# Attention in a hybrid block: turned probabilities copied out of PSUM once, low parts on GpSimd, wide score copies, heads in one stream

## The chip, the cores and the metric

The kernel runs on one core of one Trainium2 chip. The metric is the device time of one execution in microseconds. A profiled execution gives a page and a trace of one run; times inside it are counted from the start of its span. Abbreviations: PE is TensorE's matmuls and PEld its weight loads, DVE is VectorE, ACT is ScalarE, POOL is GpSimd, SP is the engine that issues DMAs.

## The reference

The whole program is a grouped convolution with attention, then a state-space block with a dense and a routed feed-forward part. The change touches only attention over the 4096 pixels of an image, in 8 heads (2 images x 4 groups) of 64 channels:

```
# qn (gated, normalized input), key_ and value: (b, g, 64, 4096) each
qf = jnp.transpose(qn.reshape(b, g, cq, h * w), (0, 1, 3, 2))
kf = jnp.transpose(key_.reshape(b, g, cq, h * w), (0, 1, 3, 2))
vf = jnp.transpose(value.reshape(b, g, cq, h * w), (0, 1, 3, 2))
scores = jnp.einsum('bgnc,bgmc->bgnm', qf, kf) * (1.0 / math.sqrt(c))   # c = 256
attn = jax.nn.softmax(scores, axis=-1)
ctx = jnp.einsum('bgnm,bgmc->bgnc', attn, vf)
```

## The kernel before

The convolution phase leaves q, k and v in DRAM, split into bf16 parts that add up to nearly f32. `attention_phase` works through 8 heads, each cut into 32 query tiles of 128 queries (`g` counts tiles over all heads). A tile has 4096 scores per query.

Scores: for each of 8 chunks of 512 keys three bf16 matmuls (L534) add up q times k in a PSUM bank of `ps_s`, which has four. VectorE copies a chunk to `prob[u]` in SBUF (L615), scaled by 1/16, and takes the chunk's maximum; after eight chunks L620 takes the negated row maximum. ScalarE takes the exponentials in place, 1024 columns at a time, with their sums (L586). `prob` has two buffers, for tiles in turn (`u`).

Values: TensorE needs the probabilities turned, keys on the partitions. For each of 8 groups `k` of 512 keys, four f32 transposes go to one of two PSUM banks `ps_t` (L543). ScalarE copies the group as bf16, the high part `hi` (L592); VectorE subtracts the high part from PSUM and writes the rest as bf16, the low part `lo` (L624). Then four pairs of matmuls (L554) take high and low parts as weights: the high part against 128 columns of `vv` (both bf16 parts of v), the low part against 64. At the end of a tile VectorE sums and inverts the row sums (L628, L630), adds the two halves of `ps_o` and scales them (L633, L635) into `oh`, which SP stores for each head.

The order on each engine is written out by hand. In round `k` of a tile, TensorE does the scores of the next tile (chunks 0 and 1 in round 0, then one chunk in rounds 1 to 6: `SCORES_AT`), the values of group `k - 2`, and the transposes of group `k`. VectorE does the score copies, in round 6 the maximum, the low part, and in round 2 the finish of the tile before. ScalarE does the high part and, after rounds 0, 2 and 4, the tile's next exponentials, after round 6 the first of the next tile. The transposes of group `k` wait for exponential `k // 2` and for the low part of group `k - 2`, whose bank they overwrite. Every head begins with its eight score chunks and a maximum, then runs its 32 tiles, and ends with its last values and finish before the next head's scores start.

Of the kernel before, what the change touches and what calls it, by code (L numbers as in the profile page):

```python
# [13 lines left out]
P = 128  # L14
# [429 lines left out]
def attention_phase(nc, ctx, ident, q_split, k_split, v_split, attn_out):  # L444

# [8 lines left out]
    hi, lo = sb("p_hi", [P, 2, CH], BF16), sb("p_lo", [P, 2, CH], BF16)  # L457
    mx, nmx = sb("mx", [P, 2, NCH]), sb("nmx", [P, 2])
# [3 lines left out]
    ps_s = ctx.enter_context(nc.psum_tensor("ps_s", [P, 4, CH], F32))  # L462
# [5 lines left out]
    t_ready, hi_ready, lo_ready, pv_done = sem("t_ready"), sem("hi_ready"), sem("lo_ready"), sem("pv_done")  # L468
    o_ready, o_stored, fin_step = sem("o_ready"), sem("o_stored"), sem("fin_step")

    LOADS = 11
    SC = L // CH
    EC = SC // 2
    TG = L // CH
    scale = 1.0 / 16.0


    SCORES_AT = (0, 0, 1, 2, 3, 4, 5, 6)

# [4 lines left out]
    def tiles(eng, head, step):

        step(head * QT, 0, 0, False, True)
        with eng.Fori(0, QT // 2 - 1) as it:
            for u in (1, 0):
                step(head * QT + it * 2 + 2 - u, it * 2 + 2 - u, u, True, True)
        step(head * QT + QT - 1, QT - 1, 1, True, False)  # L490

    def heads(eng, body):
        with eng.Fori(0, HEADS // 2) as hp:
            for j in range(2):
                body(hp * 2 + j, j, hp)

    start_semaphores()
    with nc.Block() as block:
        @block.sync
        def _(sp):  # L500
# [26 lines left out]
        @block.tensor  # L527
        def _(pe):
            def head(h, j, hp):
                def scores(g, t, u, c):  # L530

                    pe.wait_ge(s_copied, ONE + g * SC + c + 1)
                    for n, (a, b) in enumerate(((qa, ka), (qa, kb), (qb, kc))):
                        last = pe.matmul(ps_s[:, c % 4, :], a[j][:, ds(t * P, P)], b[j][:, c * CH:(c + 1) * CH],  # L534
                                         start=(n == 0), stop=(n == 2))
                    last.then_inc(s_ready, 1)

                def transposes(g, t, u, k):

                    pe.wait_ge(exp_ready, ONE + g * EC + k // 2 + 1)  # L540
                    pe.wait_ge(lo_ready, ONE + g * TG + k + 1)
                    for m in range(4):
                        last = pe.transpose(ps_t[:, k % 2, m * P:(m + 1) * P],  # L543
                                            prob[u][:, (4 * k + m) * P:(4 * k + m + 1) * P], ident[:, :])
                    last.then_inc(t_ready, 1)

                def values(g, t, u, k):

                    pe.wait_ge(lo_ready, ONE + g * TG + k + 3)
                    if k == 0:  # L550
                        pe.wait_ge(o_ready, ONE + g)
                    for m in range(4):
                        for n, (part, cols) in enumerate(((hi, P), (lo, DH))):
                            last = pe.matmul(ps_o[:, u, 0:cols], part[:, k % 2, m * P:(m + 1) * P], vv[j][:, 4 * k + m, 0:cols],  # L554
                                             start=(k == 0 and m == 0 and n == 0), stop=(k == TG - 1 and m == 3 and n == 1))
                    last.then_inc(pv_done, 1)

                def step(g, t, u, before, after):
                    for k in range(TG):
                        if after:  # L560
                            for c in range(SC):
                                if SCORES_AT[c] == k:
                                    scores(g + 1, t + 1, 1 - u, c)
                        if k >= 2:
                            values(g, t, u, k - 2)
                        elif before:
                            values(g - 1, t - 1, 1 - u, TG - 2 + k)
                        transposes(g, t, u, k)
                    if not after:
                        values(g, t, u, TG - 2)  # L570
                        values(g, t, u, TG - 1)

                pe.wait_ge(loaded[j], ONE + (hp + 1) * 16 * LOADS)
                for c in range(SC):
                    scores(h * QT, 0, 0, c)
                tiles(pe, h, step)

            heads(pe, head)

        @block.scalar  # L580
        def _(act):
# [7 lines left out]
            def his(g, k):  # L589
                act.wait_ge(t_ready, ONE + g * TG + k + 1)  # L590
                act.wait_ge(pv_done, ONE + g * TG + k + 1)
                act.activation(hi[:, k % 2, :], ps_t[:, k % 2, :], ACT.Copy).then_inc(hi_ready, 1)  # L592

            def step(g, t, u, before, after):
                if not before:
                    exps(g, u, 0)
                for k in range(TG):
                    his(g, k)
                    if k in EXPS_AT:
                        c = EXPS_AT.index(k) + 1  # L600
                        if c < EC:
                            exps(g, u, c)
                        elif after:
                            exps(g + 1, 1 - u, 0)

            act.preload_act_table(ACT.Exp)
            heads(act, lambda h, j, hp: tiles(act, h, step))

        @block.vector
        def _(dve):  # L610
            def head(h, j, hp):
                def copies(g, u, c):

                    dve.wait_ge(s_ready, ONE + g * SC + c + 1)
                    dve.tensor_scalar(prob[u][:, c * CH:(c + 1) * CH], ps_s[:, c % 4, :], scale, -FLT_MAX,  # L615
                                      ALU.mult, ALU.max, accum_out=mx[:, u, c:c + 1]).then_inc(s_copied, 1)

                def maximum(g, u):
                    dve.wait_ge(s_copied, ONE + g * SC + SC + 4)
                    dve.tensor_reduce(nmx[:, u:u + 1], mx[:, u, :], AX.X, ALU.max, negate=True).then_inc(max_ready, 1)  # L620

                def los(g, u, k):
                    dve.wait_ge(hi_ready, ONE + g * TG + k + 1)
                    dve.tensor_tensor(lo[:, k % 2, :], ps_t[:, k % 2, :], hi[:, k % 2, :], ALU.subtract).then_inc(lo_ready, 1)  # L624

                def finish(g, t, u):

                    dve.tensor_reduce(rsum[:, u:u + 1], rs[:, u, :], AX.X, ALU.add).then_inc(fin_step, 1)  # L628
                    dve.wait_ge(fin_step, ONE + g * 3 + 1)
                    dve.reciprocal(rinv[:, u:u + 1], rsum[:, u:u + 1]).then_inc(fin_step, 1)  # L630
                    dve.wait_ge(fin_step, ONE + g * 3 + 2)
                    dve.wait_ge(pv_done, ONE + (g + 1) * TG + 2)
                    dve.tensor_scalar(otmp[:, :], ps_o[:, u, DH:P], rinv[:, u:u + 1], None, ALU.mult).then_inc(fin_step, 1)  # L633
                    dve.wait_ge(fin_step, ONE + g * 3 + 3)
                    dve.scalar_tensor_tensor(oh[:, j, ds(t, 1), :].rearrange("p a c -> p (a c)"), ps_o[:, u, 0:DH],  # L635
                                             rinv[:, u:u + 1], otmp[:, :], ALU.mult, ALU.add).then_inc(o_ready, 1)

                def step(g, t, u, before, after):
                    for k in range(TG):
                        if after:  # L640
                            for c in range(SC):
                                if SCORES_AT[c] == k:
                                    copies(g + 1, 1 - u, c)
                        if after and k == MAX_AT:
                            maximum(g + 1, 1 - u)
                        los(g, u, k)
                        if before and k == FINISH_AT:
                            finish(g - 1, t - 1, 1 - u)
                    if not after:
                        finish(g, t, u)  # L650

                if j == 0:
                    dve.wait_ge(o_stored, ONE + hp * 32)
                for c in range(SC):
                    copies(h * QT, 0, c)
                maximum(h * QT, 0)
                tiles(dve, h, step)


            dve.sem_inc(s_copied, 4)  # L660
            dve.sem_inc(lo_ready, 2)
            dve.sem_inc(pv_done, 2)
            dve.sem_inc(o_ready, 1)
            heads(dve, head)


# [1580 lines left out]
```

## Time and profile before

| | |
|---|---|
| median of 3 runs | 9130.96 us (9113.76 to 9133.64) |
| the profiled execution | 9120.24 us, span 9118.2 us |
| mean granted TensorE clock | 0.948 |
| busy over the span: TensorE, VectorE, ScalarE, GpSimd | 89%, 76%, 56%, 42% |
| attention, in the profile | from about 658 to 3847 us |

The page shows the busy share of each engine over the whole span and the costliest groups of instructions. "idle before" is the time that an engine stood still ahead of the instructions of a group, and behind the arrow is what ended it. Matmuls are pipelined: one that lasts 0.22 us can start 0.08 us after another, so distances between starts say more about TensorE than durations do.

### The profile page before, as it was taken

To read this page: it belongs to the slowest core of one execution; us is meant where nothing else is said; L and a number is where in the kernel's file an instruction comes from. 1 tells how busy PE (TensorE), PEld (TensorE's weight loads), DVE (VectorE), ACT (ScalarE), POOL (GpSimd) and SP (SyncE) were. 2 spreads that over 40 slices of the span, in tenths; PEclk is the share of its full clock that TensorE was granted. 3 is DMA by queue.
4 is the path that set the end of the run, shared out by engine and by line. 5 is a ranking of instruction groups with operands and counts; after the bars stand their busy time and mean duration, and the time that the engine had idled before them with its cause. 6 is when DMAs were issued, how large, how long until landed. Compare 5 with 4: busy or idle time off the path is not lost. (4 is left out here: it accounts for less than half of the span.)

```text
span 9118.2 us, 145832 instructions
## 1 busy us (share of the span) xinstructions
PE 8092.2 (89%) x44996; PEld 4779.7 (52%) x44996; DVE 6910.1 (76%) x11667; ACT 5070.7 (56%) x8536; POOL 3849.0 (42%) x1769
## 2 busy tenths in 40 slices
PE   8969999999999999858999999999999998684993
PEld 3436666666666666633444444444444443353883
DVE  3428888888888888748998899899999999561116
ACT  2227777777777777635666666666556665221223
POOL 1000000000000000019999999999999999332005
PEclk9989999999999999969999999999999999897996
DMA  1130101011010100041111111111111111233213
GB/s 66 60 115 0 33 0 33 0 33 32 0 33 0 33 0 5 30 164 63 66 65 65 65 65 65 60 65 65 61 63 58 63 65 60 102 130 117 74 54 118
DMA packets 177488, 512.23 MB, mean 56 GB/s; under 512 B 32790, under 2 KB 71348, under 8 KB 148912
## 3 DMA queue, kind: packets, MB, share of 16 engines
q1 hardware_dynamic: 162096, 467.73, 15.5%
q10 hardware_dynamic: 8960, 25.17, 0.7%
q0 software_dynamic: 6144, 16.33, 0.5%
q14 instruction: 209, 1.71, 0.1%
q8 instruction: 79, 1.29, 0.1%
HBM read 377.49 MB, written 132.12 MB: 56 GB/s over the span
## 5 line engine op out<-in xcount | busy, mean ns | idle before, releaser
L1426 DVE TENSOR_TENSOR_SCAN hh<-mb_ps_da,state,hh 128x512 f32<-128x512 f32 x2048 | 2491.2, 1266 | 127.6 <-POOL hh L1339 73.1
L1339 POOL TENSOR_TENSOR hh<-dtx,bb 128x1024 f32<-128x1024 f32 x1024 | 2399.3, 2368 | 226.4 <-PE mb_ps_y L1088 221.8
L1229 ACT ACTIVATE mb_ps_da<-dt,amat 128x512 f32<-128x512 f32 x2048 | 1393.1, 686 | 1346.2 <-DVE hh L1426 1337.6
L1088 PE MATMUL mb_ps_y<-hh,ident 128*128 128x512 f32 x4096 | 1983.8, 612 | 18.3 <-POOL hh L1345 12.7
L534 PE MATMUL ps_s<-k,q 128*128 128x512 bf16 x6144 | 1618.3, 381 | 79.3 <-DMA v<-v_split 69.3
L624 DVE TENSOR_TENSOR p_lo<-ps_t,p_hi 128x512 bf16<-128x512 f32 x2048 | 1408.9, 688 | 330.4 <-ACT p_hi L592 329.7
L592 ACT ACTIVATE p_hi<-ps_t 128x512 bf16<-128x512 f32 x2048 | 1212.3, 592 | 754.1 <-PE ps_t L543 751.1
L1316 POOL MEMSET keep<- 128x17 f32 x1 | 0.1, 114 | 3502.6 <-POOLq L54 3502.6
L615 DVE TENSOR_SCALAR_CACHE_REDUCE prob<-ps_s 128x512 f32<-128x512 f32 x2048 | 1376.2, 682 | 61.5 <-PE ps_s L534 46.4
L543 PE MATMUL ps_t<-ident,prob 128*128 128x128 f32 x8192 | 1299.0, 281 | 9.4 <-ACT prob L586 9.4
L1088 PEld LDWEIGHTS mb_ps_y<-hh,ident 128*128 128x128 f32 x4096 | 792.9, 196 | 967.9 <-issue 858.3
L586 ACT ACTIVATE prob<-prob,nmx 128x1024 f32<-128x1024 f32 x1024 | 1170.5, 1143 | 135.8 <-DVE nmx L620 106.8
L1433 DVE TENSOR_TENSOR hh<-hh,mb_ps_c 128x1024 f32<-128x1024 f32 x768 | 923.5, 1202 | 263.2 <-PE mb_ps_c L1077 232.0
L554 PE MATMUL ps_o<-v,p_hi 128*128 128x128 bf16 x8192 | 979.5, 221 | 55.6 <-DVE p_lo L624 29.1
L554 PEld LDWEIGHTS ps_o<-v,p_hi 128*128 128x128 bf16 x8192 | 727.8, 98 | 484.3 <-DVE p_lo L624 335.1
L554 PE MATMUL ps_o<-v,p_lo 128*128 128x64 bf16 x8192 | 916.9, 193 | 0.0
L543 PEld LDWEIGHTS ps_t<-ident,prob 128*128 128x128 f32 x8192 | 863.0, 141 | 16.5 <-ACT prob L586 11.7
L534 PEld LDWEIGHTS ps_s<-k,q 128*128 (+1 forms) x6144 | 593.4, 98 | 430.1 <-issue 90.3
L554 PEld LDWEIGHTS ps_o<-v,p_lo 128*128 128x128 bf16 x8192 | 722.2, 98 | 144.9
L1345 POOL TENSOR_TENSOR hh<-hh,cc 128x1024 f32<-128x1024 f32 x256 | 606.4, 2369 | 8.7 <-ACT state L1238 8.7
L1077 PE MATMUL mb_ps_c<-xbc,pick 128*128 128x512 bf16 x768 | 302.4, 394 | 266.3 <-DVE hh L1433 265.1
L1038 PE MATMUL mb_ps_p<-mb_u,win 128*128 128x512 f32 x1024 | 503.7, 617 | 15.4 <-DMA win<-in_L_attn_in_proj_w 15.4
(229 smaller groups left out, 8272.9 us busy)
## 6 DMA issues: line engine op xcount, KB each, us to landing
bb<-mb_bc SPq DMA_DIRECT2D x128, 1024.0 KB, 4.6
cc<-mb_bc SPq DMA_DIRECT2D x256, 256.0 KB, 3.1
k<-k_split SPq DMA_DIRECT2D x48, 512.0 KB, 15.2
q<-q_split SPq DMA_DIRECT2D x32, 512.0 KB, 16.6
mb_u<-u SPq DMA_DIRECT2D x32, 512.0 KB, 3.2
m_dirs<-mo SPq DMA_DIRECT2D x32, 512.0 KB, 8.3
ex_w<-in_L_ffn_w SPq DMA_DIRECT2D x16, 1024.0 KB
k_split<-k_part SPq DMA_DIRECT2D x12, 1024.0 KB
```

What stands on the lines that cost most here:

```text
L534: last = pe.matmul(ps_s[:, c % 4, :], a[j][:, ds(t * P, P)], b[j][:, c * CH:(c + 1) * CH], start=(n == 0), stop=(n == 2))
L543: last = pe.transpose(ps_t[:, k % 2, m * P:(m + 1) * P], prob[u][:, (4 * k + m) * P:(4 * k + m + 1) * P], ident[:, :])
L554: last = pe.matmul(ps_o[:, u, 0:cols], part[:, k % 2, m * P:(m + 1) * P], vv[j][:, 4 * k + m, 0:cols], start=(k == 0 and m == 0 and n == 0 ...
L586: act.activation(prob[u][:, cs], prob[u][:, cs], ACT.Exp, bias=nmx[:, u:u + 1], accum_out=rs[:, u, c:c + 1]).then_inc(exp_ready, 1)
L592: act.activation(hi[:, k % 2, :], ps_t[:, k % 2, :], ACT.Copy).then_inc(hi_ready, 1)
L615: dve.tensor_scalar(prob[u][:, c * CH:(c + 1) * CH], ps_s[:, c % 4, :], scale, -FLT_MAX, ALU.mult, ALU.max, accum_out=mx[:, u, c:c + 1]).t ...
L624: dve.tensor_tensor(lo[:, k % 2, :], ps_t[:, k % 2, :], hi[:, k % 2, :], ALU.subtract).then_inc(lo_ready, 1)
L1088: last = pe.matmul(ps_y[:, kk, :], ident[:, :], hh[:, r % RING, kk, :], start=(r % S == 0), stop=(r % S == S - 1))
L1229: act.activation(ps_da[:, exp_bank(e), :], dt[:, j, blk, :], ACT.Exp, scale=amat[:, j, blk, r % S:r % S + 1]).then_inc(da_ready, 1)
L1339: pool.tensor_tensor(hh[:, r % RING], dtx[:, j, half(r // S)], bb[:, r % S, :].unsqueeze(1).broadcast_to([P, HK, CH]), ALU.mult).then_inc( ...
L1426: dve.tensor_tensor_scan(h, a, h, state[:, s.j, q % S, blk:blk + 1], ALU.mult, ALU.add).then_inc(scanned, 1)
L1433: dve.tensor_tensor(hh[:, r % RING], hh[:, r % RING], ps_c[:, :].unsqueeze(1).broadcast_to([P, HK, CH]), ALU.mult).then_inc(hc_dve, 1)
```

## The change

- Score copies are 1024 columns wide (`copies`, 4 per tile): `ps_s` becomes two buffers of two banks each. TensorE writes a pair of chunks (6 matmuls) before it signals, in rounds 0, 1, 2 and 4; VectorE copies in rounds 0, 1, 3 and 4, with the maximum in round 4.
- A turned group is copied out of PSUM once, as f32, to `pt`, a ring of four groups in SBUF: groups 0, 1, 3, 4 and 6 by ScalarE, 2, 5 and 7 by VectorE (`turn`).
- The high part is no tile of its own any more: it is the upper half of each f32 in `pt`, read by TensorE as every second bf16 of `hi_view`.
- GpSimd computes the low part from `pt` and that view into a ring of four (`lows`).
- Values run three groups behind the transposes (`LAG`), not two. A round is now transposes, values, scores. Transposes of group `k` wait for the copy of group `k - 2`.
- The row sum and reciprocal (`total`) are taken in round 2, the rest of the finish in round 5.
- All heads are one stream: the last tile of a head computes the scores of the next head's first tile, after a wait for that head's loads. The first two and the last two tiles of each head are written out, those between stay in a loop of two.

The scores are still three products of bf16 parts. The core of the diff:

```diff
-    ps_s = ctx.enter_context(nc.psum_tensor("ps_s", [P, 4, CH], F32))
+    ps_s = ctx.enter_context(nc.psum_tensor("ps_s", [P, 2, 2, CH], F32))
-    SCORES_AT = (0, 0, 1, 2, 3, 4, 5, 6)
-    EXPS_AT = (0, 2, 4, 6)
-    MAX_AT = 6
-    FINISH_AT = 2
+    RING = 4
+    pt = sb("p_turned", [P, RING, CH])
+    lo = sb("p_lo", [P, RING, CH], BF16)
+    LAG = 3
+    ON_ACT, ON_DVE = (0, 1, 3, 4, 6), (2, 5, 7)
+    PAIRS_AT, COPY_AT, TOTAL_AT, MAX_AT, FINISH_AT = (0, 1, 2, 4), (0, 1, 3, 4), 2, 4, 5
+    EXPS_AT = (6, 0, 2, 4)
+    hi_view = pt[:, :, :].bitcast(BF16)
...
 TensorE
+            def scores(g, t, j, p):
+                pe.wait_ge(s_copied, ONE + g * PAIR + p + 1)
+                for half in range(2):
+                    c = 2 * p + half
...
+                last.then_inc(s_ready, 1)
+            def transposes(s, k):
+                pe.wait_ge(exp_ready, ONE + s.g * PAIR + k // 2 + 1)
+                turned(pe, s.g, k - 2)
...
+            def values(g, u, j, k):
+                pe.wait_ge(lo_ready, ONE + g * TG + k + 1)
+                if k == 0:
+                    pe.wait_ge(o_ready, ONE + g + 1)
+                for m in range(4):
+                    his = hi_view[:, k % RING, 2 * m * P + 1:2 * (m + 1) * P:2]
+                    los = lo[:, k % RING, m * P:(m + 1) * P]
+                    pe.matmul(ps_o[:, u, 0:P], his, vv[j][:, 4 * k + m, :], start=(k == 0 and m == 0), stop=False)
+                    last = pe.matmul(ps_o[:, u, 0:DH], los, vv[j][:, 4 * k + m, 0:DH], start=False, stop=(k == TG - 1 and m == 3))
+                last.then_inc(pv_done, 1)
+            def step(s):
+                for k in range(TG):
+                    transposes(s, k)
+                    if k >= LAG:
+                        values(s.g, s.u, s.j, k - LAG)
+                    elif s.before:
+                        values(s.g - 1, 1 - s.u, s.jb, TG - LAG + k)
+                    if s.after:
+                        if k == 0 and s.next_head:
+                            pe.wait_ge(loaded[s.ja], ONE + (s.hpa + 1) * 16 * LOADS)
+                        for p in range(PAIR):
+                            if PAIRS_AT[p] == k:
+                                scores(s.g + 1, 0 if s.next_head else s.t + 1, s.ja, p)
...
 ScalarE
+            def turn(s, k):
+                act.wait_ge(t_ready, ONE + s.g * TG + k + 1)
+                act.wait_ge(pv_done, ONE + s.g * TG + k + 1)
+                act.activation(pt[:, k % RING, :], ps_t[:, k % 2, :], ACT.Copy).then_inc(pt_act, 1)
+            def step(s):
+                for k in range(TG):
+                    if k in ON_ACT:
+                        turn(s, k)
+                    for c in range(1, PAIR):
+                        if EXPS_AT[c] == k:
+                            exps(s.g, s.u, c)
+                    if EXPS_AT[0] == k and s.after:
+                        exps(s.g + 1, 1 - s.u, 0)
...
 GpSimd
+            def lows(s, k):
+                turned(pool, s.g, k)
+                pool.tensor_tensor(lo[:, k % RING, :], pt[:, k % RING, :], hi_view[:, k % RING, 1::2], ALU.subtract).then_inc(lo_ready, 1)
...
 VectorE
+            def step(s):
+                for k in range(TG):
+                    if k == TOTAL_AT and s.before:
+                        total(s.g - 1, 1 - s.u)
+                    if s.after:
+                        for p in range(PAIR):
+                            if COPY_AT[p] == k:
+                                copies(s.g + 1, 1 - s.u, p)
+                        if k == MAX_AT:
+                            maximum(s.g + 1, 1 - s.u)
+                    if k in ON_DVE:
+                        turn(s, k)
+                    if k == FINISH_AT and s.before:
...
+                        finish(s.g - 1, s.tb, 1 - s.u, s.jb)
+            for t, v in ((s_copied, 2), (pv_done, 4), (o_ready, 2)):
+                dve.sem_inc(t, v)
```

The last lines add a head start to three counters, so that the first waits on rings and buffers pass.

## Rows read from the trace of the kernel before

**Rows 1.** The page: busy time of each engine; two groups of VectorE.

```profile
PE 8092.2 (89%) x44996; PEld 4779.7 (52%) x44996; DVE 6910.1 (76%) x11667; ACT 5070.7 (56%) x8536; POOL 3849.0 (42%) x1769
...
L624 DVE TENSOR_TENSOR p_lo<-ps_t,p_hi 128x512 bf16<-128x512 f32 x2048 | 1408.9, 688 | 330.4 <-ACT p_hi L592 329.7
...
L615 DVE TENSOR_SCALAR_CACHE_REDUCE prob<-ps_s 128x512 f32<-128x512 f32 x2048 | 1376.2, 682 | 61.5 <-PE ps_s L534 46.4
```

**Rows 2.** Busy time by stretch (PE, PEld, DVE, ACT, POOL), granted clock, DMA share, GB/s.

```profile
640.00:3848.00 3208.00, 3109.27 (x30720) 2177.80 (x30720) 2766.90 (x7424) 2320.68 (x4096) 0.00 (x0) 0.99 0.07 18
2000.00:2244.00 244.00, 239.43 (x2403) 169.02 (x2400) 213.61 (x572) 183.04 (x324) 0.00 (x0) 1.00 0.00 0
```

**Rows 3.** Line L620: count, minimum, median, maximum ns, first and last start.

```profile
L620 DVE TENSOR_REDUCE nmx<-mx x256: 161/161/164, 666.6 to 3829.3; 128x1 f32<-128x8 f32 x128
```

**Rows 4.** Timeline inside a head: start us, duration us, engine, line, operation.

```profile
2000.67 0.22 PE L554 MATMUL ps_o<-v,p_hi 128*128 128x128 bf16 x1
...
2000.75 0.22 PE L554 MATMUL ps_o<-v,p_hi 128*128 128x128 bf16 x1
...
2002.85 0.68 DVE L615 TENSOR_SCALAR_CACHE_REDUCE prob<-ps_s 128x512 f32<-128x512 f32 x1
...
2003.57 0.16 DVE L620 TENSOR_REDUCE nmx<-mx 128x1 f32<-128x8 f32 x1
2003.68 0.69 DVE L624 TENSOR_TENSOR p_lo<-ps_t,p_hi 128x512 bf16<-128x512 f32 x1
2003.77 1.15 ACT L586 ACTIVATE prob<-prob,nmx 128x1024 f32<-128x1024 f32 x1
2003.81 1.46 PE L534 MATMUL ps_s<-k,q 128*128 128x512 bf16 x6
...
2005.11 0.22 PE L554 MATMUL ps_o<-v,p_hi 128*128 128x128 bf16 x1
...
2005.44 0.63 PE L543 MATMUL ps_t<-ident,prob 128*128 128x128 f32 x4
...
2005.91 0.81 PE L534 MATMUL ps_s<-k,q 128*128 128x512 bf16 x3
2006.12 0.60 ACT L592 ACTIVATE p_hi<-ps_t 128x512 bf16<-128x512 f32 x1 [0.62 <-PE ps_t L543]
...
2006.56 0.22 PE L554 MATMUL ps_o<-v,p_hi 128*128 128x128 bf16 x1
2006.61 1.15 ACT L586 ACTIVATE prob<-prob,nmx 128x1024 f32<-128x1024 f32 x1
...
2015.96 1.15 ACT L586 ACTIVATE prob<-prob,nmx 128x1024 f32<-128x1024 f32 x1
```

**Rows 5.** Timeline at the start of a head, in the same columns.

```profile
2251.48 9.34 PE L534 MATMUL ps_s<-k,q 128*128 128x512 bf16 x30 [3.36 <-issue]
...
2260.50 1.15 ACT L586 ACTIVATE prob<-prob,nmx 128x1024 f32<-128x1024 f32 x1 [13.67 <-DVE nmx L620]
...
2261.79 0.44 PE L543 MATMUL ps_t<-ident,prob 128*128 128x128 f32 x2 [0.97 <-ACT prob L586]
```

**Rows 6.** Who waited for whom from 2000 to 2244: us, times, longest.

```profile
PEld ps_o L554 <- DVE p_lo L624: 26.7, 63, 0.8
DVE p_lo L624 <- ACT p_hi L592: 24.6, 24, 1.2
```

**Rows 7.** Groups by line and shape: a plain copy out of PSUM to f32.

```profile
L1163 ACT ACTIVATE xpre<-mb_ps_p 128x512 f32<-128x512 f32 x128 | 74.2, 580 | 26.6 <-PE mb_ps_p L1038 26.6
```

**Rows 8.** Groups by line and shape: GpSimd's operations with two operands.

```profile
L1615 POOL TENSOR_TENSOR ml_m<-ml_m,ml_back 128x1024 f32<-128x1024 f32 x16 | 43.4, 2714 | 16.6 <-DMA ml_m<-m_dirs 16.6
...
L165 POOL TENSOR_TENSOR q_part<-resid,q_part 128x4096 bf16<-128x4096 f32 x3 | 24.8, 8266 | 0.2
```

**Rows 9.** The page: weight loads of the transposes and of the high parts.

```profile
L554 PEld LDWEIGHTS ps_o<-v,p_hi 128*128 128x128 bf16 x8192 | 727.8, 98 | 484.3 <-DVE p_lo L624 335.1
...
L543 PEld LDWEIGHTS ps_t<-ident,prob 128*128 128x128 f32 x8192 | 863.0, 141 | 16.5 <-ACT prob L586 11.7
```

More of the change, by code:

```diff
@@ L471, in attention_phase @@
     LOADS = 11
-    SC = L // CH
-    EC = SC // 2
+    PAIR = 4
     TG = L // CH
+    LAG = 3
     scale = 1.0 / 16.0
-    SCORES_AT = (0, 0, 1, 2, 3, 4, 5, 6)
-    EXPS_AT = (0, 2, 4, 6)
-    MAX_AT = 6
-    FINISH_AT = 2
[L484 to L490, printed above, removed]
@@ L492, in heads, with __init__ @@
-    def heads(eng, body):
-        with eng.Fori(0, HEADS // 2) as hp:
-            for j in range(2):
-                body(hp * 2 + j, j, hp)
+    ON_ACT, ON_DVE = (0, 1, 3, 4, 6), (2, 5, 7)
+    PAIRS_AT, COPY_AT, TOTAL_AT, MAX_AT, FINISH_AT = (0, 1, 2, 4), (0, 1, 3, 4), 2, 4, 5
+    EXPS_AT = (6, 0, 2, 4)
+    hi_view = pt[:, :, :].bitcast(BF16)
+    class Tile:
+        def __init__(s, h, j, hp, t, u, opening, closing, first=False, last=False):
+            s.h, s.j, s.hp, s.t, s.u = h, j, hp, t, u
+            s.g = h * QT + t
+            s.before, s.after = not (first and opening), not (last and closing)
+            s.jb = 1 - j if first else j
+            s.tb = QT - 1 if first else t - 1
+            s.ja = 1 - j if last else j
+            s.next_head = last
+            s.hpa = hp + j
+            s.oh_again = isinstance(t, int) and t == 1 and not opening and not (isinstance(hp, int) and hp == 0)
@@ new lines, in tiles, with heads @@
+    def tiles(eng, h, j, hp, step, opening, closing):
+        step(Tile(h, j, hp, 0, 0, opening, closing, first=True))
+        step(Tile(h, j, hp, 1, 1, opening, closing))
+        with eng.Fori(1, QT // 2 - 1) as it:
+            for u in range(2):
+                step(Tile(h, j, hp, it * 2 + u, u, opening, closing))
+        step(Tile(h, j, hp, QT - 2, 0, opening, closing))
+        step(Tile(h, j, hp, QT - 1, 1, opening, closing, last=True))
+    def heads(eng, step):
+        tiles(eng, 0, 0, 0, step, True, False)
+        tiles(eng, 1, 1, 0, step, False, False)
+        with eng.Fori(1, HEADS // 2 - 1) as hp:
+            for j in range(2):
+                tiles(eng, hp * 2 + j, j, hp, step, False, False)
+        tiles(eng, HEADS - 2, 0, HEADS // 2 - 1, step, False, False)
+        tiles(eng, HEADS - 1, 1, HEADS // 2 - 1, step, False, True)
@@ L578, in _ @@
-            heads(pe, head)
+                        last = pe.matmul(ps_s[:, p % 2, half, :], a[j][:, t * P:(t + 1) * P] if isinstance(t, int) else a[j][:, ds(t * P, P)],
+                                         b[j][:, c * CH:(c + 1) * CH], start=(n == 0), stop=(n == 2))
+                last.then_inc(s_ready, 1)
[3 more added lines that the diff above has]
+                for m in range(4):
+                    last = pe.transpose(ps_t[:, k % 2, m * P:(m + 1) * P],
+                                        prob[s.u][:, (4 * k + m) * P:(4 * k + m + 1) * P], ident[:, :])
+                last.then_inc(t_ready, 1)
@@ new lines, in step @@
+            def step(s):
[11 more added lines that the diff above has]
+                                scores(s.g + 1, 0 if s.next_head else s.t + 1, s.ja, p)
+                if not s.after:
+                    for k in range(LAG):
+                        values(s.g, s.u, s.j, TG - LAG + k)
@@ L580, in _ @@
+            pe.wait_ge(loaded[0], ONE + 16 * LOADS)
+            for p in range(PAIR):
+                scores(0, 0, 0, p)
+            heads(pe, step)
         @block.scalar
@@ L606, in _ @@
-            act.preload_act_table(ACT.Exp)
-            heads(act, lambda h, j, hp: tiles(act, h, step))
+            def turn(s, k):
[3 more added lines that the diff above has]
+            def step(s):
+                for k in range(TG):
+                    if k in ON_ACT:
+                        turn(s, k)
[4 more added lines that the diff above has]
+                        exps(s.g + 1, 1 - s.u, 0)
@@ L609, in _ @@
+            act.preload_act_table(ACT.Exp)
+            exps(0, 0, 0)
+            heads(act, step)
+        @block.gpsimd
+        def _(pool):
+            def lows(s, k):
[3 more added lines that the diff above has]
+                for k in range(TG):
+                    lows(s, k)
+            heads(pool, step)
         @block.vector
@@ L610, in _ @@
         def _(dve):
[L611 to L657, printed above, removed]
@@ L660, in _, with copies @@
[L660 to L664, printed above, removed]
+            def copies(g, u, p):
+                dve.wait_ge(s_ready, ONE + g * PAIR + p + 1)
+                dve.tensor_scalar(prob[u][:, 2 * p * CH:2 * (p + 1) * CH], ps_s[:, p % 2, :, :].rearrange("p a n -> p (a n)"), scale, -FLT_MAX,
+                                  ALU.mult, ALU.max, accum_out=mx[:, u, p:p + 1]).then_inc(s_copied, 1)
@@ L667, in tokens_phase @@
+            for t, v in ((s_copied, 2), (pv_done, 4), (o_ready, 2)):
+                dve.sem_inc(t, v)
+            for p in range(PAIR):
+                copies(0, 0, p)
+            maximum(0, 0)
+            heads(dve, step)
 def tokens_phase(nc, ctx, ident, x, attn_out, t1, u1):
```

96 lines of the change are left out of this document (37 added, 59 removed).

## The prediction

> **What bounds the kernel now.** I read the page first. TensorE is busy 89% of the span and VectorE 76% [rows 1], but its forty slices mix stages, and the change touches one of them. The table by stretches gives that one: attention takes the 3.2 ms from 640 to 3848, with TensorE busy 3109 us of 3208, VectorE 2767, ScalarE 2321 and GpSimd idle [rows 2]. The times of the row maximum (L620, one per query tile) give its beat: 256 maxima from 666.6 to 3829.3 are 255 intervals in 3162.7 us, 12.40 us each on average [rows 3]. Within a head the beat is shorter: the exponential that follows the maximum starts at 2003.77 and next at 2015.96, 12.19 us later [rows 4], and the same interval recurs 29 more times in this head, 12.18 on average. The rest sits between heads, where the pipeline drains: 3.36 us of issue before TensorE's first scores of a head at 2251.48, and its first turned group only at 2261.79 [rows 5].
>
> Then the timeline, for the distances between starts on TensorE. Call T four transposes, V four pairs of value products, S the three score products of 512 columns. A double S to V is 5.11 - 3.81 = 1.30, V to T 0.33 or 0.34, T to S 0.47, one S to V 0.65 [rows 4]. So eight rounds of T, V, S need 8 x (0.47 + 0.34 + 0.65) = 11.68 us without any wait. The other 0.50 of the beat are waits, and the list of waits for the 20 beats of the steady stretch says for what: V's weights for the low parts of VectorE, and these for the high parts of ScalarE [rows 6]. TensorE's own work is therefore a floor close below: whatever the change takes from VectorE, steady tiles can gain 0.50 x 256 = 128 us at most, and the heads' ends (12.40 - 12.18) x 255 = 56.
>
> **The change, part by part.**
>
> *Copies and low parts.* VectorE does eight score copies of 0.682 and eight low parts of 0.688 per tile [rows 1]. After the change: four copies of 1024 columns, three plain copies of turned probabilities, none of the low parts. No wide copy with a maximum is in the trace. From the start of a 512-wide one to the start of the maximum are 0.72 us (2002.85 to 2003.57) [rows 4]. The 512 further columns cost at most a second copy, 0.68, and, if ScalarE's step from 512 to 1024 columns (0.580 for a copy, 1.15 for the exponential) is the measure, 0.57 [rows 4, 7]. For VectorE I take a little less, 0.53, since a part of its 0.682 is fixed (half as many fixed parts is what the wide form saves), so 1.25 us from the wide copy's start to the maximum's. VectorE is busy 213.6 us of the steady 244, 10.7 per beat, ScalarE 183.0, 9.1 [rows 2]. VectorE loses five slots of 0.6 and four fixed parts of about 0.1, to 7.3; ScalarE three of 0.5, to 7.6. Neither is a bound by its sum any more. The plain copy of 512 columns to f32 has its like in another stage, that 0.580 of ScalarE; for VectorE's I take the low part's 0.69.
>
> *GpSimd* gets eight low parts per tile. The same kinds of operand with 4096 columns take 8.27 us, which is 1.03 for 512; an f32 one of 1024 columns takes 2.71 where GpSimd is slowest, which is 1.36 for 512 [rows 8]. I take 1.20, near the middle, with ends 1.03 and 1.36. Sum 9.6 us per tile, hidden while it stays under the beat: 1.56 us each would be the limit at the beat found below. The tightest place is the fifth low part; it is ready 0.2 us before its V (below).
>
> *The order of the tile.* TensorE now does T V S S in rounds 0, 1, 2 and 4 and T V in 3, 5, 6 and 7. From T0 = 0, with the distances above: T1 2.11, T2 4.22, T3 6.33, T4 7.14, S6 and S7 from 7.95 to 9.25, T5 9.25, T6 10.06, T7 10.87, next T0 11.68, if nothing waits. Two chains do not fit into that.
>
> First, through VectorE. The last scores are readable 0.16 after 9.25 (a double S lasts 1.46 and holds the next start for 1.30), the wide copy starts 0.05 later, at 9.46; the maximum starts at 10.71, and the copy of turned group 5, queued behind it, 0.11 later at 10.82 [rows 4]. It ends 0.69 after, and T7, which waits for it (`turned(k - 2)`), starts at about 11.56 and not 10.87. V4 behind it ends at 12.37. That alone makes 12.37.
>
> Second, through ScalarE. T6 starts at 10.06. A turned group is copied 0.68 after the start of its T (2005.44 to 2006.12), the exponential queued behind that copy starts 0.49 later (2006.12 to 2006.61) [rows 4], and T follows an exponential's start by 1.29 (2260.50 to 2261.79) [rows 5]. The first exponential of the next tile is queued behind the copy of group 6 (`EXPS_AT[0] = 6`), so it starts at 11.23, though its maximum is there at about 10.91, and the next T0 comes at 11.23 + 1.29 = 12.52. Behind it stand V5 and S0 of TensorE. In the kernel before, the last scores stood in round 6 but T0 came only after two more score groups and V6, a double S (1.30) later in the queue, and the same chain was covered. The new beat is then 12.52, of which 0.84 us are waits.
>
> The rest of the walk has room: T4 waits for the copy of group 2 until 6.76 (it starts at 7.14), T6 for exponential 3 until 9.60 (10.06), and low part 5 ends at 11.56 + 1.20 = 12.76, V5 wants it at 12.99. GpSimd's queue then runs behind by up to 1.4 us and catches up in the long rounds.
>
> *Heads without a drain.* The boundary becomes an ordinary tile: by the code a head's loads are issued when the head two before it is stored, almost a whole head (390 us) ahead, so the new wait on them, which has scores and all later T queued behind it, costs nothing; without that cover it would cost a load. More straight code per head could bring back an issue gap of 3.4 us [rows 5] at up to 14 loop entries: 0 to 47 us; I take 0, since loop edges inside a head show none now. So all 255 intervals become 12.52: 3192.6 against 3162.7, +29.9 us.
>
> *Ends.* The first maximum comes 0.5 us later behind a wide copy; the last tile has no scores, and GpSimd's eight low parts in a row (9.6 us) end it about 1.5 us later. +2.
>
> *Strided weights.* The high part is now read as every second bf16 of the f32 copy, as TensorE's weights. A pair of value products holds 0.08 to 0.09 us now (2000.67 to 2000.75, four in a V of 0.34), hardly more than its 192 columns at the pace of S (0.65 for 1536) would take, 0.081: the loads are hidden [rows 4]. Nothing in the trace loads strided weights. The nearest row is the f32 weight of the transposes, 141 ns against 98 for bf16 [rows 9]. Ends: 0, and 0.043 us per high part, unhidden; no gain, since the passes stay. I take 0. Between the two it would be paid 24 times before T6.
>
> The Trainium skill ("TensorE: Matmul & The Clock Gate", section "Weight-path perf modes — Fast Weight Load (FWL) and DoubleRow") says that the fast load reads its four chunks of columns packed or strided, up to a step of 1,024 elements. By that rule strided loads add nothing, and the sum stays; no run here shows it yet. The sum uses 0 because the row's difference is one of type.
>
> **Sum.** 29.9 + 2 = +32 us on the profiled execution's 9120.2, 9152. The median of the runs is 9131.0, 10.8 above it; the prediction is 9131 + 32 = 9163 us.
>
> **The rivals.**
>
> *TensorE comes near its floor (faster).* If a wide copy or the exponential behind it releases its waiter earlier than by my distances, say at the beat of 12.18 that steady tiles have now, only the drains are saved: 9131 - 56 = 9075; at the floor of 11.68 it is 9131 - 184 = 8947. It decides from a beat of 12.40: below it the change is a gain. For it: VectorE and ScalarE lose over 1 us a tile each. Against: two separate chains give 12.37 and 12.52, from distances that repeat in every tile.
>
> *The first chain alone (no change).* Beat 12.37: -8 + 2, 9125.
>
> *Strided weights cost (slower).* At 0.025 per high part, what a load as slow as a pass of 128 columns (0.054 at the pace of S) sticks out from behind a pass of 64 (0.027), 24 x 0.025 = 0.6 us per tile, beat 13.12: 9131 + 185 = 9316; at 0.043 it is 13.55, 9426.
>
> *GpSimd is the bound (slower).* Low parts over 1.56 us. At 1.75 the beat is 14.0: 9131 + 410 = 9541. Against: the slowest row makes 1.36 of 512 columns; for: the strided second operand has no row. The Trainium skill ("SBUF — State Buffer", section "Who interferes with whom") says that VectorE blocks GpSimd only in a two-port mode or with two SBUF inputs; every large VectorE operation here reads PSUM, so by that rule GpSimd is not slowed and this rival loses weight. The trace of before has no attention work on GpSimd to show it.
>
> **How the numbers follow.** My walk 0.52, first chain alone or the like 0.06, near the floor 0.20, strided weights 0.15, GpSimd 0.07. What a measurement of this kernel tells from no change is about 0.2%, 18 us, a beat of 12.33 to 12.47. My walk with 0.1 us of error in the beat (and an issue gap or two) falls within it in 0.15 of its 0.52. So same 0.15 + 0.06 = 0.21, slower 0.37 + 0.15 + 0.07 = 0.59, faster 0.20. Range: from 9070, the steady beat kept and drains gone, to 9320, the strided loads at 0.025; outside are the floor, 0.043 and the GpSimd bound.
>
> **What would show it.** Right: maxima 12.5 us apart, also across heads; T0 waiting for the exponential and T7 for VectorE's copy; GpSimd at 1.2 us a low part, busy about 77%; pairs at 0.085 us. Wrong: waits of V's weights for GpSimd (its bound), pairs at 0.11 with no waits (strided loads), or a beat of 11.7 to 12.2 with T0 not waiting.

## The result and the profile after

The changed kernel takes 9152.15 us (median of 12 runs, 9143.83 to 9162.33) against 9128.58 us for the kernel before (12 runs): 1.0027 of its time, 95% interval 1.0019 to 1.0036. It is slower by 23.6 us, a quarter of a percent, though VectorE and ScalarE have less to do (776 and 403 us less over the span), and the heads no longer drain. The forecast was 32 us slower.

The engines' busy time on the page of the changed kernel, and three of its groups:

```profile
PE 7988.7 (87%) x44329; PEld 4880.3 (53%) x44996; DVE 6133.9 (67%) x8339; ACT 4667.2 (51%) x7768; POOL 5923.5 (65%) x3817
...
L640 POOL TENSOR_TENSOR p_lo<-p_turned 128x512 bf16<-128x512 f32 x2048 | 2075.8, 1040 | 1304.3 <-DVE p_turned L663 1030.2
...
L653 DVE TENSOR_SCALAR_CACHE_REDUCE prob<-ps_s 128x1024 f32<-128x1024 f32 x1024 | 1251.6, 1222 | 1156.2 <-PE ps_s L561 1156.2
...
L663 DVE COPY p_turned<-ps_t 128x512 f32<-128x512 f32 x768 | 531.2, 692 | 44.5 <-PE ps_t L570 14.2
```

Against [rows 1], VectorE falls from 6910 to 6134 us and GpSimd rises from 3849 to 5924. The idle time tells more. VectorE now stands still 1156 us before the score copies, for TensorE; in the kernel before it was 61.5 us. The engine that was relieved now waits: the tile turns at another's pace.

The row maximum (L658), in the columns of [rows 3], and the busy time by stretch, in those of [rows 2]:

```profile
L658 DVE TENSOR_REDUCE nmx<-mx x256: 156/157/158, 667.3 to 3851.0; 128x1 f32<-128x4 f32 x128
```

```profile
2000.00:2244.00 244.00, 229.34 (x2309) 173.09 (x2346) 151.89 (x314) 147.56 (x256) 159.12 (x157) 1.00 0.00 0
```

255 intervals take 3183.7 us, 12.485 each, where [rows 3] had 12.40. Inside a head they are 12.47; before, they were 12.18. TensorE is busy 229.3 of 244 us and was 239.4 [rows 2], at the same granted clock of 1.00.

The waits of the same stretch, longest first, against [rows 6]:

```profile
ACT p_turned L620 <- PE ps_t L570: 96.8, 98, 2.4
DVE prob L653 <- PE ps_s L561: 86.5, 60, 1.9
POOL p_lo L640 <- DVE p_turned L663: 78.7, 39, 2.2
PEld ps_t L570 <- DVE p_turned L663: 15.6, 20, 0.8
PE ps_t L570 <- DVE p_turned L663: 12.6, 20, 0.6
```

TensorE's waits for low parts are gone. In their place it waits, once in each of the 20 tiles, for a copy of a turned group on VectorE: T7, by 0.63. The timeline of that place, columns as in [rows 4]:

```profile
1999.42 1.23 DVE L653 TENSOR_SCALAR_CACHE_REDUCE prob<-ps_s 128x1024 f32<-128x1024 f32 x1 [1.62 <-PE ps_s L561]
...
2000.67 0.60 ACT L620 ACTIVATE p_turned<-ps_t 128x512 f32<-128x512 f32 x1 [1.16 <-PE ps_t L570]
2000.69 0.16 DVE L658 TENSOR_REDUCE nmx<-mx 128x1 f32<-128x4 f32 x1
...
2000.85 0.69 DVE L663 COPY p_turned<-ps_t 128x512 f32<-128x512 f32 x1
2001.16 1.14 ACT L614 ACTIVATE prob<-prob,nmx 128x1024 f32<-128x1024 f32 x1
...
2001.60 0.66 PE L570 MATMUL ps_t<-ident,prob 128*128 128x128 f32 x4 [0.63 <-DVE p_turned L663]
2001.62 2.04 POOL L640 TENSOR_TENSOR p_lo<-p_turned 128x512 bf16<-128x512 f32 x2 [1.84 <-DVE p_turned L663]
...
2002.54 0.65 PE L570 MATMUL ps_t<-ident,prob 128*128 128x128 f32 x4
```

Both chains of the prediction stand here side by side. On VectorE: wide copy, maximum, copy of group 5, and T7 at 2001.60. On ScalarE: the copy of group 6 at 2000.67, the exponential behind it at 2001.16 (the maximum was there at 2000.85), T0 of the next tile at 2002.54. The list of waits names only the first: T0 follows V4 by 0.11 more than a T behind a V elsewhere, too little to be shown as a wait for the exponential.

The sum of attention, in the profiled executions: 255 intervals 21.0 us longer, the first maximum 0.7 later, the last finish 12.9 after the last maximum and 13.4 before, so +21.2. The two profiled spans lie 42 us apart; the other half arose behind attention, in code that the change does not touch, and the medians lie 23.6 apart. That half is most likely scatter: from the last maximum to the end of the span the kernel before takes 5289 us, the changed one 5310, and x1 to x6 and x8, with the same code there, 5285 to 5298. Single runs of the changed kernel are up to 18.5 us apart, and this profile belongs to the longest of them.

### The profile page after: what moved, and what is told of

It is laid out like the page before. It is cut to its first block and busy times, and to the rows that moved or that the text cites. A ratio compares the mean times of both kernels' runs of the same rounds, so it can differ in the third digit from the quotient of the medians.

```text
span 9160.6 us, 142325 instructions
## 1 busy us (share of the span) xinstructions
PE 7988.7 (87%) x44329; PEld 4880.3 (53%) x44996; DVE 6133.9 (67%) x8339; ACT 4667.2 (51%) x7768; POOL 5923.5 (65%) x3817
## 5 line engine op out<-in xcount | busy, mean ns | idle before, releaser
L640 POOL TENSOR_TENSOR p_lo<-p_turned 128x512 bf16<-128x512 f32 x2048 | 2075.8, 1040 | 1304.3 <-DVE p_turned L663 1030.2
L653 DVE TENSOR_SCALAR_CACHE_REDUCE prob<-ps_s 128x1024 f32<-128x1024 f32 x1024 | 1251.6, 1222 | 1156.2 <-PE ps_s L561 1156.2
L561 PE MATMUL ps_s<-k,q 128*128 128x512 bf16 x5634 | 1387.5, 380 | 96.5 <-DMA v<-v_split 69.6
L620 ACT ACTIVATE p_turned<-ps_t 128x512 f32<-128x512 f32 x1280 | 764.5, 597 | 1274.8 <-PE ps_t L570 1274.8
L570 PEld LDWEIGHTS ps_t<-ident,prob 128*128 128x128 f32 x8192 | 942.5, 141 | 423.5 <-DVE p_turned L663 186.7
L582 PE MATMUL ps_o<-v,p_turned 128*128 128x128 bf16 x8192 | 971.6, 220 | 0.9 <-POOL p_lo L640 0.9
L561 PEld LDWEIGHTS ps_s<-k,q 128*128 (+1 forms) x6144 | 531.5, 98 | 557.3 <-DMA v<-v_split 69.4
L582 PEld LDWEIGHTS ps_o<-v,p_turned 128*128 128x128 bf16 x8192 | 749.3, 98 | 1.2 <-POOL p_lo L640 1.2
L663 DVE COPY p_turned<-ps_t 128x512 f32<-128x512 f32 x768 | 531.2, 692 | 44.5 <-PE ps_t L570 14.2
L1078 PE MATMUL mb_ps_p<-xpre,cwd 128*128 128x512 f32 x1024 | 505.0, 618 | 44.1 <-DVE cwd L1502 17.9
```

Of the source, the lines that this page charges most:

```text
L561: last = pe.matmul(ps_s[:, p % 2, half, :], a[j][:, t * P:(t + 1) * P] if isinstance(t, int) else a[j][:, ds(t * P, P)], b[j][:, c * CH:(c ...
L570: last = pe.transpose(ps_t[:, k % 2, m * P:(m + 1) * P], prob[s.u][:, (4 * k + m) * P:(4 * k + m + 1) * P], ident[:, :])
L582: pe.matmul(ps_o[:, u, 0:P], his, vv[j][:, 4 * k + m, :], start=(k == 0 and m == 0), stop=False)
L640: pool.tensor_tensor(lo[:, k % RING, :], pt[:, k % RING, :], hi_view[:, k % RING, 1::2], ALU.subtract).then_inc(lo_ready, 1)
L653: dve.tensor_scalar(prob[u][:, 2 * p * CH:2 * (p + 1) * CH], ps_s[:, p % 2, :, :].rearrange("p a n -> p (a n)"), scale, -FLT_MAX, ALU.mult ...
L1078: last = pe.matmul(out, lhsT, rhs, start=start, stop=stop)
```

## The experiments

All are made from the changed kernel. Walk positions are us after T0, the tile's first transposes.

**x1: the first chain taken away.** The copy of group 5 goes from VectorE to ScalarE.

```diff
-    ON_ACT, ON_DVE = (0, 1, 3, 4, 6), (2, 5, 7)
+    ON_ACT, ON_DVE = (0, 1, 3, 4, 5, 6), (2, 7)
```

> After the change, with the copy of turned group 5 moved from VectorE to ScalarE (ScalarE: 0, 1, 3, 4, 5, 6; VectorE: 2, 7). Nothing is left out. This takes away the first chain (T7 waits for VectorE's copy behind the maximum) and leaves the second (first exponential of the next tile queued behind ScalarE's copy of group 6). My theory: the beat between maxima stays at 12.47, since the second chain sets it; T7's wait of 0.63 vanishes and T0 waits for the exponential instead by about 0.7; time 9152. Rival, that T7's wait sets the beat: it falls by the 0.63, to about 11.9, time about 9000.

The waits from 2000 to 2244, and the row maximum:

```profile
PEld ps_t L570 <- issue: 18.0, 20, 0.9
PE ps_t L570 <- ACT prob L614: 15.1, 20, 0.8
```

```profile
L658 DVE TENSOR_REDUCE nmx<-mx x256: 157/157/159, 666.7 to 3847.4; 128x1 f32<-128x4 f32 x128
```

The beat stayed at 12.47 (most frequent interval; average 12.473). T7's 0.63 is gone and T0 waits 0.76 for the exponential instead. TensorE's longest wait in the list of after was worth nothing by itself. One run of 9138.7 us.

**x2: the second chain taken away.** Group 6 goes from ScalarE to VectorE.

```diff
-    ON_ACT, ON_DVE = (0, 1, 3, 4, 6), (2, 5, 7)
+    ON_ACT, ON_DVE = (0, 1, 3, 4), (2, 5, 6, 7)
-    PAIRS_AT, COPY_AT, TOTAL_AT, MAX_AT, FINISH_AT = (0, 1, 2, 4), (0, 1, 3, 4), 2, 4, 5
+    PAIRS_AT, COPY_AT, TOTAL_AT, MAX_AT, FINISH_AT = (0, 1, 2, 4), (0, 1, 3, 4), 2, 4, 6
```

> After the change, with the copy of group 6 moved from ScalarE to VectorE, behind that of group 5 (ScalarE: 0, 1, 3, 4; VectorE: 2, 5, 6, 7), and the finish one round later. Nothing is left out. This takes away the second chain and leaves the first. My theory: the beat falls only from 12.47 to 12.38, where T7's wait and the work behind it end, time 9152 - 23 = 9129. Rival, that the exponential alone sets the beat: it would fall to 12.19 (maximum at 10.62 after T0, 0.20 to the exponential, 1.37 to T), time 9081.

The waits, in the same stretch:

```profile
ACT prob L614 <- DVE nmx L658: 27.4, 20, 1.4
...
PE ps_t L570 <- DVE p_turned L663: 13.7, 19, 0.7
```

ScalarE now stands ready 1.4 us before the maximum, and TensorE waits for VectorE's copy again. The beat is 12.40 (most frequent interval), 0.02 above the expectation, and far from the 12.19 of the rival; one run, 9125.3 us. So taking away one chain alone frees little: with only the second the beat is 12.47, with only the first 12.40.

**x3: both taken away,** by exchanging groups 5 and 6.

```diff
-    ON_ACT, ON_DVE = (0, 1, 3, 4, 6), (2, 5, 7)
+    ON_ACT, ON_DVE = (0, 1, 3, 4, 5), (2, 6, 7)
-    PAIRS_AT, COPY_AT, TOTAL_AT, MAX_AT, FINISH_AT = (0, 1, 2, 4), (0, 1, 3, 4), 2, 4, 5
+    PAIRS_AT, COPY_AT, TOTAL_AT, MAX_AT, FINISH_AT = (0, 1, 2, 4), (0, 1, 3, 4), 2, 4, 6
```

> After the change, with groups 5 and 6 exchanged: ScalarE copies 0, 1, 3, 4, 5, VectorE 2, 6, 7, finish one round later. Nothing is left out. Both chains lose the copy that stood in them; what is left is scores, wide copy, maximum, exponential, T0. My theory: 12.19 (10.62 + 0.20 + 1.37), time 9152 - 71 = 9081. If instead GpSimd or strided weights had a share in the beat, it would stay above 12.3.

The waits, in the same stretch, and the row maximum:

```profile
PE ps_t L570 <- ACT prob L614: 8.8, 18, 0.5
ACT prob L614 <- DVE nmx L658: 8.5, 20, 0.4
```

```profile
L658 DVE TENSOR_REDUCE nmx<-mx x256: 157/157/158, 668.4 to 3779.1; 128x1 f32<-128x4 f32 x128
```

12.20 at its most frequent, 12.199 on average; one run, 9079.1 us, expected 9081. What is left is the bare chain: the exponential waits for the maximum, T0 for the exponential. GpSimd and the strided weights have no share in the beat of after.

**x4: the exponential ahead of the copy in ScalarE's queue.**

```diff
-    EXPS_AT = (6, 0, 2, 4)
+    EXPS_AT = (5, 0, 2, 4)
```

> After the change, with the first exponential of the next tile put ahead of ScalarE's copy of group 6 (round 5, not 6). Nothing is left out. My theory: the exponential starts at 10.82 after T0 as soon as the maximum is there, but group 6 is then copied from 11.97 to 12.57, and T0, which waits for that copy too, comes at 12.64: beat 12.64, time 9152 + 44 = 9196, slower. Rival, that the late exponential alone is the cost: 12.2 and 9081.

The waits, in the same stretch:

```profile
ACT prob L614 <- DVE nmx L658: 27.4, 20, 1.4
PEld ps_t L570 <- DVE p_turned L663: 15.6, 20, 0.8
PE ps_t L570 <- DVE p_turned L663: 12.6, 20, 0.6
PEld ps_t L570 <- ACT p_turned L620: 4.0, 19, 0.2
```

Slower: beat 12.59 (12.64 expected), one run of 9181.3 us (9196 expected). The exponential blocks ScalarE's queue for 1.4 us while it waits for the maximum, and the copy of group 6 behind it is what T0 then waits for (last row, which the list of after does not have). The remedy is not an earlier place in the queue, but another queue or an earlier maximum.

**x5: the maximum earlier.** The last scores come one round earlier, and so does what follows them; VectorE and ScalarE exchange groups 6 and 7, and the finish comes one round later.

```diff
-    ON_ACT, ON_DVE = (0, 1, 3, 4, 6), (2, 5, 7)
-    PAIRS_AT, COPY_AT, TOTAL_AT, MAX_AT, FINISH_AT = (0, 1, 2, 4), (0, 1, 3, 4), 2, 4, 5
-    EXPS_AT = (6, 0, 2, 4)
+    ON_ACT, ON_DVE = (0, 1, 3, 4, 7), (2, 5, 6)
+    PAIRS_AT, COPY_AT, TOTAL_AT, MAX_AT, FINISH_AT = (0, 1, 2, 3), (0, 1, 3, 4), 2, 4, 6
+    EXPS_AT = (4, 0, 2, 3)
```

> After the change, with the last pair of scores in round 3 (not 4), exponential 3 in round 3 and the next tile's first in round 4, ahead of later copies; ScalarE copies groups 0, 1, 3, 4, 7, VectorE 2, 5, 6; finish one round later. Nothing is left out. By the same walk: scores end at 8.33 after T0, wide copy 8.54, maximum 9.79, exponential 9.99, so T0 could come at 11.36; TensorE's own work ends at 11.5 (rounds with a double S take 2.07 in the trace of after, the others 0.79). My theory: beat 11.5, TensorE without waits, time 9152 - 0.98 x 255 = 8902. Rival, that some other wait (GpSimd's low parts, strided weights, a copy on VectorE) takes over: beat between 11.8 and 12.2, time 8980 to 9080.

The busy time by stretch, the end of a tile in the timeline, and the row maximum:

```profile
2000.00:2244.00 244.00, 238.52 (x2455) 183.25 (x2495) 160.65 (x334) 156.78 (x270) 167.97 (x166) 0.99 0.13 31
```

```profile
2005.71 0.16 DVE L658 TENSOR_REDUCE nmx<-mx 128x1 f32<-128x4 f32 x1
...
2005.90 1.15 ACT L614 ACTIVATE prob<-prob,nmx 128x1024 f32<-128x1024 f32 x1 [0.42 <-DVE nmx L658]
...
2006.63 0.64 PE L570 MATMUL ps_t<-ident,prob 128*128 128x128 f32 x4
...
2007.45 0.63 PE L570 MATMUL ps_t<-ident,prob 128*128 128x128 f32 x4
```

```profile
L658 DVE TENSOR_REDUCE nmx<-mx x256: 157/157/159, 667.2 to 3614.7; 128x1 f32<-128x4 f32 x128
```

T0 comes at 2007.45, 0.82 after T7, with no wait, though the exponential began at 2005.90. The beat is 11.53, and the time 8912.9 us (median of 5; 8902 expected), 0.9771 of the kernel before, interval 0.9757 to 0.9784. It is the fastest version here that computes the whole result, 2.3% under the kernel before, and it has every part of the change. The data path was sound; its order, three lines of the kernel, cost it the gain.

**x6: the stride of the weights by itself,** on x5, where TensorE has no wait that could hide a cost.

```diff
-                    his = hi_view[:, k % RING, 2 * m * P + 1:2 * (m + 1) * P:2]
+                    his = lo[:, k % RING, m * P:(m + 1) * P]
```

> The kernel of the run before it, with the high part's weights read from the packed low part instead of every second bf16 of the f32 copy: same count and size of all instructions, but the high part is left out of the products, so the output is not the reference's. It prices the stride alone where TensorE has no waits to hide it. My theory, strided loads cost nothing: beat and pairs (0.085) the same within 0.03 us per tile. Rival, they cost 0.025 each: 32 x 0.025 = 0.8 us less per tile here, over 200 us in all.

Three of the four high-part products of a group in x5 (first fence, strided) and of this run (second fence, packed), from the timelines:

```profile
2004.68 0.22 PE L582 MATMUL ps_o<-v,p_turned 128*128 128x128 bf16 x1
...
2004.76 0.22 PE L582 MATMUL ps_o<-v,p_turned 128*128 128x128 bf16 x1
...
2004.93 0.22 PE L582 MATMUL ps_o<-v,p_turned 128*128 128x128 bf16 x1
```

```profile
2004.45 0.22 PE L582 MATMUL ps_o<-v,p_lo 128*128 128x128 bf16 x1
...
2004.53 0.22 PE L582 MATMUL ps_o<-v,p_lo 128*128 128x128 bf16 x1
...
2004.70 0.22 PE L582 MATMUL ps_o<-v,p_lo 128*128 128x128 bf16 x1
```

Both go 0.25 in three pairs, and both beats are 11.53; the one run took 8904.6 us. 8192 strided loads cost nothing that is seen. The Trainium skill ("TensorE: Matmul & The Clock Gate", section "Weight-path perf modes — Fast Weight Load (FWL) and DoubleRow") lets the fast load take a strided pattern; this trace agrees, at a step of two bf16: in x5 and x6 the loads last 98 ns, strided or packed.

**x7: the low parts back on VectorE,** from the same copy in SBUF. GpSimd's block is taken out, and VectorE ends each round with:

```diff
                     if k in ON_DVE:
                         turn(s, k)
+                    turned(dve, s.g, k)
+                    dve.tensor_tensor(lo[:, k % RING, :], pt[:, k % RING, :], hi_view[:, k % RING, 1::2], ALU.subtract).then_inc(lo_ready, 1)
```

> After the change, with the low parts computed by VectorE (from the same f32 copy in SBUF, at the end of each round) and GpSimd idle. Nothing is left out. It undoes one part: what GpSimd carries. VectorE's sum becomes 7.3 + 8 x 0.6 = 12.1 us per tile, and it waits for ScalarE's copies in its queue ahead of score copies. My theory: it becomes the bound, beat 13 to 14, time 9290 to 9540. If it stays at 12.5, moving the low parts to GpSimd bought nothing in this schedule.

The busy time by stretch:

```profile
2000.00:2244.00 244.00, 219.01 (x2197) 164.66 (x2232) 233.58 (x449) 139.03 (x241) 0.00 (x0) 1.00 0.00 0
```

VectorE is busy 233.6 of 244 us, 96%, and sets a beat of 13.11; one run of 9303.1 us. So the move to GpSimd is worth 0.64 us a tile even in the schedule of after, and it was not what cost time. VectorE's own work is 12.6 us of each tile here, so with the copies shared out in this way the new data path needs GpSimd. Low parts on VectorE with more of the copies on ScalarE, which is busy 139 us, were not tried.

**x8: waits against constants.** Twelve more tiles of the first head are written out.

```diff
-        with eng.Fori(1, QT // 2 - 1) as it:
+        straight = 12 if opening else 0
+        for t in range(2, 2 + straight):
+            step(Tile(h, j, hp, t, t % 2, opening, closing))
+        with eng.Fori(1 + straight // 2, QT // 2 - 1) as it:
```

> After the change, with 12 more tiles of the first head written out, so that their waits are against constants and not registers. Nothing is left out. In the trace of after, written-out tiles of the first heads take 12.38 us and those in the loop 12.47. My theory, the wait of T0 against a register's value answers 0.08 us later: the first 14 or so intervals are all 12.38, and the time is about 1 us less. Rival, it is something of the head's ends: they stay at 12.47 but for the last two of a head.

The maxima where the written-out tiles end and the loop begins:

```profile
829.43 0.16 DVE L661 TENSOR_REDUCE nmx<-mx 128x1 f32<-128x4 f32 x1
...
841.82 0.16 DVE L661 TENSOR_REDUCE nmx<-mx 128x1 f32<-128x4 f32 x1
...
854.28 0.16 DVE L661 TENSOR_REDUCE nmx<-mx 128x1 f32<-128x4 f32 x1
...
866.72 0.16 DVE L661 TENSOR_REDUCE nmx<-mx 128x1 f32<-128x4 f32 x1
```

12.39, then 12.46 and 12.44. The 13 intervals before are 12.37 to 12.39; in after only the second interval of this head and those at its end are. The one run, 9136.6 us, cannot show the expected microsecond. Other intervals narrow the cause down. The tiles at the ends of heads 2 to 5 of after are straight code too, but stand in the outer loop over head pairs, and run 12.44 to 12.48, but for the one at its jump. In x2 and x3 the same tiles as in after are 0.08 faster (12.32 and 12.11), in x5, where TensorE waits for nothing, both kinds run 11.53, and in x4 the written-out ones are the slower (12.65 for 12.59). So straight code is not enough, and the 0.08 appears only where TensorE waits; that a wait against a register's value answers later fits all but x4, and is not shown.

**x9: how near GpSimd is.** Four more operations per tile, into a spare tile.

```diff
                 turned(pool, s.g, k)
+                if k >= 4:
+                    pool.tensor_tensor(spare[:, k - 4, :], pt[:, k % RING, :], hi_view[:, k % RING, 1::2], ALU.subtract)
                 pool.tensor_tensor(lo[:, k % RING, :], pt[:, k % RING, :], hi_view[:, k % RING, 1::2], ALU.subtract).then_inc(lo_ready, 1)
```

> After the change, with four more GpSimd operations per tile: the low parts of groups 4 to 7 are first computed into a spare tile, then as before. Nothing is left out. It asks how near GpSimd is to setting the beat. At 1.02 us each GpSimd has 12.2 us of work, under the beat of 12.47. My theory: the place counts, not the sum. Low part 5 starts at 11.55 after T0, when VectorE's copy is done, and now ends at 13.6, where V5 wants it at 12.96: V5 waits 0.66 and the beat is 13.1, time 9152 + 0.65 x 255 = 9318. Rival, that the sum alone counts: beat 12.47, time 9152.

The waits, in the same stretch:

```profile
PEld ps_o L583 <- POOL p_lo L643: 13.8, 18, 0.8
PE ps_t L571 <- DVE p_turned L666: 11.4, 18, 0.6
PE ps_o L583 <- POOL p_lo L643: 9.5, 18, 0.5
```

The beat is 13.17 and the time 9325.4 us, against 13.1 and 9318 expected. One run. TensorE waits for a low part once in each of the 18 tiles. GpSimd is busy 223.8 of the 244 us, 12.1 per tile, which would have fitted into 12.47. The low part of group 5 did not allow it: the added operation ahead of it cannot start before VectorE's copy is done.

## Why the prediction was right

Point by point, by its own steps.

- *The beat.* 12.52 was forecast, 12.47 came. T6 stood at 9.92 after T0, not at 10.06: rounds with a double S take 2.07 to 2.12 and those without 0.78 or 0.79, for 2.11 and 0.81. The exponential started 0.49 after the copy before it, as forecast, and T0 followed 1.37 (in the loop) or 1.29 behind, where 1.29 was forecast. So the walk was 0.14 too late at T6 and 0.08 too early at T0; that these nearly cancel is luck, the chain itself is not.
- *The two chains.* The first alone was put at 12.37; x2, which leaves only it, gave 12.40. The second was put at 12.52; x1, which leaves only it, gave 12.47. x3 took both away and landed on what the remaining distances say.
- *The floor.* TensorE's own work was put at 11.68 a tile. It is less: x5 turns at 11.53 with no wait in the tile, for the same shorter rounds. The forecast does not hang on it, but the rival at the floor (8947 us) was placed too high; x5's order reaches 8913.
- *The wide copy.* 1.25 was taken from its start to the maximum's; it is 1.27 (1999.42 to 2000.69), its duration 1.22. The choice of 0.53 for the further 512 columns, below the row of ScalarE, was right (1.222 - 0.682 = 0.54).
- *GpSimd.* 1.20 was taken for a low part, between 1.03 and 1.36; it is 1.04, at the low end, which the row with the same kinds of operands had said [rows 8]. The strided second operand costs nothing that is seen: the operands of that row are packed. Busy 65% of the steady stretch (159.1 of 244), not 77%.
- *Strided weights* at nothing: x6 shows it.
- *Heads without a drain.* Forecast as 255 equal intervals. All but one are within 0.3 of the beat; one, at 2262, is 18.58. The gain from the boundaries is 52.2 us (excess over steady intervals 3162.7 - 255 x 12.18 = 56.8 before, 3183.7 - 255 x 12.467 = 4.6 after, 12.467 being the average inside the middle heads); 56.8 was forecast, with 0 to 47 us of issue gaps as the bound, of which one came. The timeline of after at that place:

```profile
2267.69 1.11 PE L570 MATMUL ps_t<-ident,prob 128*128 128x128 f32 x4 [3.32 <-issue]
...
2269.66 0.63 PE L561 MATMUL ps_s<-k,q 128*128 128x512 bf16 x1 [0.22 <-issue]
```

It is the one backward jump of the outer loop over head pairs. TensorE had nothing for 3.32 us, and the work behind it ran slow: four transposes last 1.11 and not 0.64, which is 6 us in all with the gap. The slow part is TensorE's clock. The busy time behind the gap in the columns of [rows 2], the granted clock third from the end, first of after, then of x6:

```profile
2268.00:2272.00 4.00, 3.78 (x18) 2.33 (x18) 0.00 (x0) 1.72 (x3) 1.04 (x1) 0.50 0.02 4
```

```profile
2150.00:2154.00 4.00, 3.07 (x31) 2.32 (x33) 0.80 (x1) 2.09 (x4) 1.04 (x1) 1.00 0.02 6
```

In after the granted clock is 0.50 from 2268 to 2272, the lower of its two levels (1.2 GHz for 2.4), and 1.00 again from 2274. In x6 TensorE stood still for 3.02 us at the same jump, the clock stayed at 1.00, the transposes behind it last 0.65, and the boundary costs 3.2 us and not 6.1. In the other runs made from after it fell, and the boundary costs 3.7 to 6.0. The prediction had a price for the gap and none for the clock behind it.

- *The ends.* +2 was forecast, +0.2 came. The term for the last tile was too large: in a row low parts start 1.00 apart and not 1.20 (eleven of them take 11.02 us from 3851.86), so the last tile's eight are 8.0 and not 9.6 us.
- *The sum.* Steady tiles (12.467 - 12.18) x 255 = +73.2, boundaries -52.2, ends +0.2: +21.2, where 86.7 - 56.8 + 2 = +32 was forecast. The terms missed by 13.5 and 4.6 in opposite directions, which brought the sum nearer than its parts. The beat from which the sign turns, 12.40, lay only 0.1 below the forecast, and the result came out on the forecast side of it by 0.07.

## What to carry to other kernels

Taking work off a busy engine shortens nothing when the tile turns on a loop through several engines' queues: walk that loop by the distances between starts, and find which operation stands in a queue ahead of the one that closes it. Two chains within 0.1 us of each other hide one another, and the list of waits can show only the one that comes first in the tile, so remove both in one trial before judging either of them. A sum of busy time under the beat says nothing about a burst: ask for each operation when it can start and when it is wanted. Where work behind a gap is slow, look at the granted clock before looking for another cause.

## What the runs showed of the hardware

- A low part on GpSimd (512 columns, f32 less strided bf16, to bf16) takes 1.04 us beside a busy VectorE, and in a row they start 1.00 apart, close to the share of the 4096-column row (8.27 / 8 = 1.03). VectorE's wide copies and plain copies out of PSUM ran beside it at 1.222 and 0.692 us, and at 1.220 and 0.687 in x7, where GpSimd was idle. The Trainium skill ("SBUF — State Buffer", section "Who interferes with whom") says that only two-port modes or two SBUF inputs on VectorE contend with GpSimd; the trace agrees for operations that read PSUM, and that the named ones do contend is not shown here.
- The same low part on VectorE with two SBUF operands takes 0.689 (x7), as it did from PSUM (0.688), two thirds of GpSimd's time.
- The backward jump of the outer loop costs TensorE 3.32 us of issue in after and 3.02 in x6. Behind it the granted clock was 0.50 from 2268 to 2272 in after (four transposes in 1.11 for 0.64 us) and 1.00 in x6 (0.65 us). Jumps of the inner loop over two tiles show no gap.
- Where TensorE waits for another engine once a tile, written-out tiles run 12.38 and looped ones 12.46 on average over two, in the same head and on the same chain (after; 12.32 and 12.40 in x2, 12.11 and 12.19 in x3). Without a wait both run 11.53 (x5). The cause is open.
